# Graph attention and experts on one core: both biases folded into the weight rows, right-row splitting on VectorE, eight groups gathered ahead

## The reference

```python
x_n = layernorm(x)                           # 6250 x 256, mean 0 in every row
x_l = x_n @ W_l + b_l ; x_r = x_n @ W_r + b_r
g = leaky_relu(x_r[dst] + x_l[src], 0.2)     # 8 heads of 32
alpha = einsum('ehc,hc->eh', g, att) + log(edge_weight)
alpha = softmax of alpha over the edges of one destination
x = x + segment_sum(x_l[src] * alpha, dst) + bias
x = x + experts(layernorm(x))                # top 2 of 8 experts, 256 -> 512 -> 256, exact gelu
```

## Time and profile before

| | us |
|---|---|
| median of 3 runs | 1837.55 |
| lowest and highest run | 1829.25, 1840.62 |
| the profiled execution, its own time | 1838.26 |
| its span in the trace | 1836.2 |
| busy: TensorE, VectorE, GpSimd, ScalarE | 1707.7, 1424.2, 1269.1, 1251.3 |

### The profile page before, as it was taken

The page is one execution under the profiler, slowest core; times in us unless marked ns, Lnnn a source line. Parts: engine busy times, 40 slices in busy tenths (PEclk is TensorE's granted clock), DMA queues, the critical chain, the costliest instruction groups (busy, mean ns, idle before and its releaser), DMA issues. The chain is left out here.

```text
span 1836.2 us, 33955 instructions
## 1 busy us (share of the span) xinstructions
PE 1707.7 (93%) x8553; PEld 1293.6 (70%) x8554; DVE 1424.2 (78%) x2704; ACT 1251.3 (68%) x3138; POOL 1269.1 (69%) x1320
## 2 busy tenths in 40 slices
PE   6686899999999999999999999999797899999998
PEld 4564466666666666666666666666596799999998
DVE  6467799999999999999999999999868433333333
ACT  4520589999999999999999999987770133233222
POOL 2457767777777777777777777776435677777775
PEclk9898999999999999999999999998857999999999
DMA  6468878888888877787878878774674344444444
GB/s 213 89 190 287 248 234 245 247 240 246 240 238 241 239 238 240 239 249 235 240 238 241 244 238 245 238 232 131 195 250 167 74 76 69 71 71 69 70 73 52
DMA packets 208385, 352.60 MB, mean 192 GB/s; under 512 B 43978, under 2 KB 97524, under 8 KB 208101
## 3 DMA queue, kind: packets, MB, share of 16 engines
q1 hardware_dynamic: 144037, 201.90, 33.9%
q0 software_dynamic: 63072, 147.92, 33.6%
q10 hardware_dynamic: 1120, 1.05, 0.2%
HBM read 302.77 MB, written 47.98 MB: 191 GB/s over the span
## 5 line engine op out<-in xcount | busy, mean ns | idle before, releaser
L761 POOL DMA_INDIRECT rows<-left_rows,srcs x880 | 841.8, 957 | 270.9 <-issue 255.0
L1313 PEld LDWEIGHTS p_gain<-W,hots 128*128 128x128 f32 x1760 | 330.7, 192 | 225.4 <-issue 147.7
L1313 PE MATMUL p_gain<-W,hots 128*128 128x264 f32 x1760 | 473.5, 394 | 8.8 <-DVE acc L1087 7.7
L1251 PE MATMUL p_row<-rows,ident 128*128 128x512 f32 x880 | 461.0, 608 | 21.0 <-DMA rows<-left_rows,srcs 20.1
L1767 ACT ACTIVATE e_hT<-e_ph,b_column 128x128 f32<-128x128 f32 x420 | 120.1, 369 | 325.0 <-PE e_ph L1792 325.0
L1138 ACT ACTIVATE L<-p_row 128x512 f32<-128x512 f32 x440 | 261.4, 594 | 93.4 <-PE p_row L1251 89.8
L1208 ACT ACTIVATE far<-iota_row,dl 128x128 f32<-128x128 f32 x880 | 298.8, 390 | 0.0
L1243 PE MATMUL p_row<-rights,hotT 128*128 128x256 f32 x1760 | 280.2, 301 | 16.6 <-DMA rights<-right_rows 10.3
L967 DVE TENSOR_TENSOR L<-L,p_weights 128x1024 f32<-128x1024 f32 x220 | 265.9, 1209 | 12.2 <-ACT L L1138 12.2
L982 DVE TENSOR_REDUCE raw<-L 128x32 f32<-128x1056 f32 x220 | 272.8, 1240 | 1.3
L1058 DVE TENSOR_TENSOR W<-rows,p_weights 128x1024 f32<-128x1024 f32 x220 | 266.3, 1210 | 5.3 <-PE p_gain L1313 1.2
(11 more groups left out here) (255 smaller groups left out, 1855.6 us busy)
## 6 DMA issues: line engine op xcount, KB each, us to landing
rights<-right_rows SPq DMA_DIRECT2D x440, 256.0 KB
locals<-item_locals SPq DMA_DIRECT2D x110, 256.0 KB, 3.9
rows<-left_rows,srcs POOLq DMA_INDIRECT x880
right_rows<-p_parts SPq DMA_DIRECT2D x49, 256.0 KB, 2.6
w<-in_L_ffn_W SPq DMA_DIRECT2D x16, 512.0 KB, 6.3
X<-in_x SPq DMA_DIRECT2D x8, 896.0 KB, 4.9
left_rows<-p_y SPq DMA_DIRECT2D x49, 132.0 KB, 1.8
normed_rows<-acc SPq DMA_DIRECT2D x7, 896.0 KB, 4.8
```

The costliest lines, as they stand in the source:

```text
L761: nc.gpsimd.indirect_dma_start(out=s["rows"][:, g % RINGS, n, :], out_offset=None, in_=d["left"][:, :], in_offset=bass.IndirectOffsetOnAxi ...
L1251: nc.tensor.matmul(p_row[:, n, :].rearrange("p (m f) -> p m f", f=D), s["ident"][:, :], rows[:, g.slot(RINGS), PAIR * n:PAIR * (n + 1), 0: ...
L1313: last = nc.tensor.matmul(p_gain[:, n, 0:D + H], hots[:, g.slot(2), i, :], W[:, g.slot(2), i, :, :].rearrange("p h c -> p (h c)"), start=( ...
```

## The change

- *Biases in the weights.* The sum of a normalised row is zero. ScalarE now normalises with a shift larger by 1, so that every row of the left operand has the sum 256, and `fold_bias` adds (bias - column sum of W) / 256 to every row of the weights. The product then holds the bias. The column sums are made by TensorE with a matrix of ones (`sum_columns`): the left one ahead of the first transpose, the right one after left tile 3. VectorE folds the left bias in before it makes the head columns, the right one at tile 4.
- *Left loop.* No bias additions on either engine; VectorE copies its 264 columns by one operation. GpSimd waits for `items_done` and issues the 21 index gathers in a row.
- *Right loop.* VectorE takes the high and the low part of every tile, of even tiles out of PSUM, of odd tiles out of a copy that ScalarE makes. GpSimd has no subtractions and issues gathers alone, 8 groups instead of 6, as soon as all left rows are stored. TensorE waits for the low part (even) or for ScalarE's copy (odd) of the tile four back.
- *SP.* The read of the node tiles moves from left tile 26 to right tile 6, and with it five DMAs that stood at right tile 2.
- *ScalarE* takes the logarithm of the weights at right tile 4.

```diff
-EARLY_GROUPS = 6
+EARLY_GROUPS = 8
-ITEMS_READ, GATHER_AT = 16, 9
...
-                pool.wait_ge(operands_done, 3)
-                for t in range(0, NODE_TILES, 2):
-                    pool.wait_ge(left_by_scalar, t // 2 + 1)
-                    nc.gpsimd.tensor_tensor(y[:, t % 4, 0:D], y[:, t % 4, 0:D], side_bias[:, 0, :], ALU.add).then_inc(left_biased, 1)
-                    if t == ITEMS_READ:
-                        pool.wait_ge(items_done, 1)
-                    if t >= ITEMS_READ:
-                        for i in range((t - ITEMS_READ) // 2 * 4 // 3, min(3 * QI, (t + 2 - ITEMS_READ) // 2 * 4 // 3)):
-                            read_rows(i)
+                pool.wait_ge(items_done, 1)
+                for i in range(3 * QI):
+                    read_rows(i)
...
-                for t in range(1, NODE_TILES, 2):
-                    pool.wait_ge(right_steps, 2 * t + 2)
-                    wait(pool, right_stored[t % 4], 16 * (t // 4))
-                    nc.gpsimd.tensor_tensor(parts[:, t % 4, 1, :], right[:, t % 4, :], parts[:, t % 4, 0, :], ALU.subtract
-                                            ).then_inc(low_by_pool, 1)
-                    if t == GATHER_AT:
-                        pool.wait_ge(turned_copied, QI)
-                        for k in range(4):
-                            pool.wait_ge(left_stored[k], 16 * len(range(k, NODE_TILES, 4)))
-                    if t >= GATHER_AT:
-                        gather((t - GATHER_AT) // 2)
-                for i in range((NODE_TILES - GATHER_AT) // 2, EARLY_GROUPS * G):
+                pool.wait_ge(turned_copied, QI)
+                for k in range(4):
+                    pool.wait_ge(left_stored[k], 16 * len(range(k, NODE_TILES, 4)))
+                for i in range(EARLY_GROUPS * G):
                     gather(i)
...
                 def project_right(t):
                     if t < 4:
                         pe.wait_ge(*left_copied(NODE_TILES + t - 4))
+                    elif t % 2:
+                        pe.wait_ge(right_by_scalar, (t - 3) // 2)
                     else:
-                        pe.wait_ge(right_steps, 2 * (t - 4) + 1)
+                        pe.wait_ge(low_done, t - 3)
...
+                def sum_columns(side):
+                    for h in range(KD):
+                        last = nc.tensor.matmul(ps[:, side, 0:D], s["ones"][:, :], W[:, h, side, 0:D], start=(h == 0), stop=(h == KD - 1))
+                    last.then_inc(sums_done, 1)
...
-                    if t == 26:
-                        sp.wait_ge(stored, 16 * 4)
-                        sp.dma_start(s["jrow"][0:1, :], d["node_tile"].rearrange("n o -> o n")[:, ::PAIR],
-                                     allow_slow_non_contiguous=True).then_inc(row_in, 16)
...
-                    if t == 2:
+                    if t == 6:
                         sp.wait_ge(stored, 16 * 6)
+                        sp.dma_start(s["jrow"][0:1, :], d["node_tile"].rearrange("n o -> o n")[:, ::PAIR],
+                                     allow_slow_non_contiguous=True).then_inc(row_in, 16)
...
+                for t in range(NODE_TILES):
+                    if t % 2:
+                        act.wait_ge(right_projected, t + 1)
+                        wait(act, low_done, t - 3)
+                        nc.scalar.activation(right[:, t % 4, :], py[:, right_slot(t), 0:D], ACT.Copy).then_inc(right_by_scalar, 1)
...
-                    nc.vector.scalar_tensor_tensor(shift[:, tiles_of(b)], mv[:, tiles_of(b), 0], -1.0, std[:, 2, tiles_of(b)],
-                                                   ALU.mult, ALU.mult).then_inc(scaled, 1)
+                    step(nc.vector.tensor_tensor(shift[:, tiles_of(b)], mv[:, tiles_of(b), 0], std[:, 2, tiles_of(b)], ALU.mult))
+                    nc.vector.tensor_scalar(shift[:, tiles_of(b)], shift[:, tiles_of(b)], -1.0, 1.0, ALU.mult, ALU.add).then_inc(scaled, 1)
+
+                def fold_bias(side):
+                    v.wait_ge(sums_done, side + 1)
+                    step(nc.vector.scalar_tensor_tensor(side_bias[:, side, :], ps[:, side, 0:D], -1.0, side_bias[:, side, :], ALU.mult, ALU.add))
+                    for h in range(KD):
+                        last = nc.vector.scalar_tensor_tensor(W[:, h, side, 0:D], side_bias[:, side, :], 1.0 / D, W[:, h, side, 0:D],
+                                                              ALU.mult, ALU.add)
+                    return last
...
-                    nc.vector.tensor_copy(y[:, t % 4, D:DL], py[:, t % 4, D:DL])
-                    nc.vector.tensor_tensor(y[:, t % 4, 0:D], py[:, t % 4, 0:D], side_bias[:, 0, :], ALU.add).then_inc(left_by_vector, 1)
-
-                def take_right(t):
-                    v.wait_ge(right_projected, t + 1)
-                    if t >= 4 and t % 2:
-                        v.wait_ge(*low_of(t - 4))
-                    nc.vector.tensor_tensor(right[:, t % 4, :], py[:, right_slot(t), 0:D], side_bias[:, 1, :], ALU.add
-                                            ).then_inc(right_steps, 1)
+                    nc.vector.tensor_copy(y[:, t % 4, :], py[:, t % 4, 0:DL]).then_inc(left_by_vector, 1)
```

64 lines of the change are left out of this document (36 added, 28 removed).

## The result

The changed kernel takes 1823.92 us (median of 11 runs, 1820.59 to 1826.32) where the kernel before, timed beside it, takes 1838.47 (11 runs, 1829.25 to 1841.71). The ratio is 0.9925, interval [0.9912, 0.9937]: 14 us or 0.75% faster, which is under the 1% that the prediction named as the bound. The profiled execution took 1823.1 us, span 1821.4, against a span of 1836.2.

What follows compares the result with a forecast made beforehand. GpSimd was taken to set the pace of the edges from about 400 us, so only their earlier start could win: -8.8 + 1.5 + 1.5 - 6.4 = -12.2, from 1838.3 to 1826.1 us, range 1813 to 1841.

Steps and rivals of the forecast that it cites:

- Left loop, gathers: Preparing stage, left tiles: index gathers issued back to back end ScalarE's waits for source and destination rows; -8.8 us.
- The two places: Left loop, products of tiles 30 to 33 and 38 to 42, at ScalarE's two waits: 3.4 and 5.4 us won.
- The clog: Left loop, 54 to 61 us: some 11 more gathers run against the node tiles' element writes; +1.5 us, bounds 0 and +17.
- the start: Start of the preparing stage: column sums and bias folds delay the first left products; +1.5 us, bounds 0 and +3.5.
- the hole: Left loop, about 54 us: everything waits for stores of left rows; expected to stay about 8 us on TensorE.
- The slower rival: Left loop, element writes: each of 17 gathers that joins adds about 1 us; +3.3 in all, 1842 us, chance 0.08.
- They stand behind 896 single-element writes.: Left loop, 54 to 61 us: stores of left rows wait behind the node tiles' element writes, with 16 DMA engines full.
- Right loop, -6.4: Preparing stage, right tiles: VectorE stops being the limit, stores come next; 64 us against 70.4, head included.
- the third rival: Gathers push stores back in left and right loops, only the right loop's head is won: -5.7, 1833 us, chance 0.19.
- Eight early groups, 0: Edges: eight instead of six groups gathered ahead only lengthen GpSimd's wait before group 16; 0, bounds 0 and -10 us.
- SP's order, 0: Node-tile read moves from left tile 26 to right tile 6; last use is the preparing stage's end, so 0.
- What would show it: Signs: no ScalarE index-row waits, full clock 70 to 105 us, right pairs 1.9 to 2.1 us, GpSimd wait 12 to 16.

Runs made afterwards that it cites:

- the paced kernel: Changed kernel with the 21 index gathers held back to the old pace, no bias additions brought back; ratio to the kernel before 0.9948.
- the kernel with rows: Changed kernel with node tiles written as 128 descriptors of 28 bytes instead of 896 of 4; ratio to the kernel before 0.9870.
- the one with the other queue: Changed kernel with the same 896 node-tile element writes issued by ScalarE on its own queue; ratio to the kernel before 0.9894, on a slower chip.

## Why the prediction was right, and where it was lucky

The forecast was 1826.0, the time 1823.9. Its sum was -12.2, and -14.5 was measured (-14.8 in the spans). Two terms are off by 3 us each, in opposite directions, and that they cancel is luck; so are the last 1.1 us, from stages that nobody touched.

- **Left loop, gathers, -8.8.** Right in mechanism: both waits went, and TensorE ran at its own pace behind them at the full clock. It measured -9.9. The two places gave 4.1 and 6.0 us for 3.4 and 5.4: the sum let the cast on ScalarE cost TensorE all its 0.95 us each time, and it cost some 0.4. GpSimd's order alone gave 7.4 to 7.7 in the kernels that put it back; what gave the rest is not shown.
- **The clog, +1.5, and the start, +1.5.** Together they measured -0.1 in the profiled execution. The clog is mis-sized: 12 gathers were issued before the hole's end instead of 4 (11 more were forecast), and it was no longer (7.05 us for 7.43, and 7.26 with four gathers in the paced kernel). The step that failed is the price per packet: in the hole, with full engines, the added packets cost nothing. The rule of the Trainium skill that the prediction names (DMA: Bandwidth & Descriptors, Queues, rings and completion order) would have made it 4.6 us; it did not show. The start was about right: the product of tile 24 came 0.7 us later, and 2.2 and 1.3 in the two kernels with fewer early groups and the same left loop. That so little of it is left behind the hole here (-0.1, where those two have +1.6 and +1.2) is luck of one execution. The slower rival had its price of 1 us per gather from landing times of 8.2 us, which were a symptom.
- **"They stand behind 896 single-element writes."** The elements are the cause, as the kernel with rows shows; "behind" is wrong, as the one with the other queue shows.
- **Right loop, -6.4.** Mis-sized: -3.3. VectorE's pair came out at 1.53 us for 1.49, and stores did come next, as said. The 64 us became 66.2, and the loop before was counted as 70.4 where 69.4 passed between the marks used here. The sum took 354 GB/s for the whole loop; the trace has that only late (357 GB/s from 144 to 150 us) and 216 to 263 between 102 and 120. The pace while gathers run is what it had wrong: 1.07 us a tile forecast, 1.51 measured (30 tiles from 100.48 to 145.71 us). The total came near 64 because the sum had put 13 us beside that pace. -3.3 is about what the third rival gave the loop, "no quicker than now", with 3 us from its head. What makes the stretch slow stays open: moving the small reads to another queue or making 1792 of them 256 didn't help, and most of the other small packets were never tried.
- **Eight early groups, 0.** Right: 15.8 us of wait where 12 to 16 were forecast, 1086.4 for 1086.7 us of edges, first weighing 59.9 us after the start (60 to 61 forecast). That the edges gain nothing came out; what the eight gathers cost the right loop, about 2 us by the kernels with six and four groups, is in the term above.
- **SP's order, 0.** No wait in the traces points at it. No run put the read of the node tiles back in the left loop, so it is not tested.
- **What would show it.** The right pairs were not 1.9 to 2.1 us while gathers ran but between 1.45 and 5.8, in fits, 3.0 in the mean. This sign failed. No wait for index rows, the full clock from 70 to 94 us, GpSimd's wait and the edges' own length came out.

## What to carry to other kernels

Here a write of 896 single numbers to memory was paid by all stores for microseconds after its packets were gone, in either queue that was tried; lay the numbers side by side first, even if the read then picks them singly. In the left loop a gather that was early cost nothing, and one that landed after its user was due cost its lateness and the slow products behind it; so move it by the place of its user, not to be earliest. Where the next stage has a ring that limits how far ahead one may run, count what the ring lets through before filling it: the rest gained nothing here and made the right loop some 2 us longer per two groups.

## What the runs showed of the hardware that was not expected

- 896 writes of 4 bytes passed in about 2 us, and for some 8 us after, packets of about 1 KB held an engine for 0.64 us instead of 0.042. Eight more gathers in that time cost nothing (a hole of 7.05 us with 12, 7.26 with 4).
- 1792 reads of 4 bytes, made 256 of 28 bytes, changed nothing that the spread of the right loop lets one see (63.37 for 62.90 us, on two chips).
- A gather of 128 rows costs the right loop an estimated 0.28 us (62.65, 60.32 and 58.08 us with 32, 24 and 16 of them, one execution each), for 1.25 us of GpSimd.
- Three chips run the kernel before in 2237 to 2254 us instead of 1838 to 1842, with nearly the same duration of each instruction on VectorE and ScalarE in the edges (VectorE's weighing 1213 for 1210 ns), and TensorE idle for up to 10 us at a time.
